# Attention with a mixture-of-experts layer on one core: softmax sums divide the pairs' outputs, their reciprocals transposed with the next pair

## The chip, the cores and the metric

The kernel runs on one core of a Trainium2 chip. Its engines run side by side, each through its own queue in program order, and wait for one another on semaphores: TensorE (PE in the profile, PEld its weight loads), VectorE (DVE), ScalarE (ACT), GpSimd (POOL) and SyncE (SP), which only issues transfers. The metric is the time of one execution on the device in microseconds, the median of three runs.

## The reference

For x of shape (8, 256, 128), all in fp32, the result is x + attention(xn) + experts(xn), with xn the layer norm of x. What matters here is the attention part:

```python
sim = einsum('bhid,bhjd->bhij', q, k) * 8 + slopes * bias   # 16 heads of 64, j over 2 null keys + 256
sim = where(causal, -neg, sim)
attn = softmax(sim, axis=-1)
out = einsum('bhij,bhjd->bhid', attn, v)
out = out.transpose(0, 2, 1, 3).reshape(b, n, h * dh) @ Wout
```

q comes from a second layer norm of xn, k and v from xn itself; q and k are scaled to unit length. The expert part is a shared expert and the two best of eight experts for each token.

## The kernel before

There are four stages. Up to about 90 us the inputs are loaded, weights are transposed and split into a high and a low part (so that three reduced-precision matmuls replace one in fp32), tokens are routed, and POOL scatters them to expert slots in HBM. Up to about 180 us the experts run over 40 tiles. Then comes the attention loop over 8 batches of 256 tokens (written out for the first and the last, a hardware loop for the six between), which takes two thirds of the span, and a drain of 9 slots.

A batch has 16 slots, one for each head h. The function entry is written once for each engine and goes through the slots s; head_at(part, s, lag) gives the head that an engine works on in slot s at a given lag. Heads come in pairs (p = h // 2). For head h:
- PE, slot h (even only): scores of both heads of the pair into banks 0 and 1 (L1095).
- DVE, slot h: adds the bias, takes the row minimum of the negated scores (L902).
- ACT, slot h+1: exponential, with the row sum into den (L658). It waits also for the null copies of the pair two before.
- DVE, slot h+2: reciprocal of the sums (L882), and two scalings of the probabilities by it (L886), for the rows of the two token tiles.
- POOL, slot h+2 (odd only): copies the probabilities of the two null keys aside for the pair (L493), after the norm work of that slot.
- PE, slot h+3: three transpositions of the scaled probabilities into bank 2 (even head) or 3 (odd) (L1086), ahead of the scores of its slot. DVE (L894) or ACT (L646) copies 384 columns to probT.
- PE, slot 2p+5: probabilities times values of the pair into bank 4 (L1076, L1077).
- ACT and DVE, slot 2p+6: split of that output into a high part (L638) and a low part (L877).
- PE, slot 2p+7: output projection by three matmuls (helper three, L953 to L955), summed over the pairs in bank 6.

Beside the heads, each slot holds up to two side jobs of the lists JOBS: "kq" (projections of keys or queries of the next batch, 128x512), "tr" (their transposition, L1041), "v" (values), "sh" (shared expert), "pn" (null probabilities transposed), "yt" (result transposed and summed with the gathered expert rows). A kq job goes from PE in slot s to ACT (L596, L597), DVE (L863, L867) and POOL in slot s+1: POOL raises to the power -0.5 (L424 for keys; L427 and L430 for queries) and scales 128x512 (L440). Such jobs stand in PE's slots 1, 4, 5, 6, 7, 11, 12 and 13, so in POOL's slots 2, 5, 6, 7, 8, 12, 13 and 14. POOL also splits inputs into two parts in slots 0, 1 and 2 (L455, L458, L475, L478) and the shared expert's product in slots 7 and 10 (L466, L468), and in slot 10 it waits for the end of the batch before (fin) and issues four gathers of expert rows (L504).

The order on POOL within a slot is: input splits, norm work, null copies, gathers. The slots' order on each engine is that of the program text; nothing reorders it.

## Time and profile before

| | |
|---|---|
| median of 3 runs | 546.41 us (544.74 to 547.65) |
| the profiled execution | 547.41 us, span 545.5 us, mean granted clock 0.951 |
| PE busy | 432.8 us (79%) |
| DVE busy | 406.6 us (75%) |
| ACT busy | 364.5 us (67%) |
| POOL busy | 327.7 us (60%) |
| attention loop | from about 182 us to the end |

Busy PE time uses modelled ends, since matmuls overlap. The granted clock of TensorE has two levels here, 1.00 (2.4 GHz) and 0.50 (1.2 GHz). In a timeline row "[1.40 <-DVE nmx L902]" says that the engine stood idle for 1.40 us before the instruction and what ended it. POOL's durations are rough.

### The profile page before, as it was taken

What the parts mean: (1) busy time and instruction counts of PE and PEld (TensorE: products, weight loads), DVE (VectorE), ACT (ScalarE), POOL (GpSimd) and SP (SyncE); (2) the same over time, 40 slices, a digit from 0 to 9 for tenths busy, and PEclk for the clock granted to TensorE, in tenths of its full rate; (3) what the DMA queues carried; (4) which work ended last, traced back from release to release, by engine and by line L of the source; (5) the groups of instructions that cost most, each with busy time, mean ns of one, the idle gap of its engine ahead of it and who ended that gap; (6) DMA issues with size and microseconds to landing.
All of it is one profiled execution on the core that took longest, in us unless ns stands there. A gap on an engine that the chain in (4) does not pass through costs nothing.

```text
span 545.5 us, 12308 instructions
## 1 busy us (share of the span) xinstructions
PE 432.8 (79%) x2867; PEld 319.2 (59%) x2868; DVE 406.6 (75%) x1469; ACT 364.5 (67%) x1096; POOL 327.7 (60%) x492
## 2 busy tenths in 40 slices
PE   0657243888888789987997998999799899889895
PEld 0656121667666557665765766666576566567663
DVE  3855532655554499989988998898898899888885
ACT  1343132566555778886895887888588688769854
POOL 2276778910000478867957867786796787677140
PEclk9999666999999999999998998999899899989989
DMA  7931112122221000001000000100000000010010
GB/s 221 351 113 40 38 48 68 40 70 63 61 59 51 18 0 22 2 2 29 11 0 19 19 0 0 38 0 0 24 15 0 19 19 0 0 37 2 3 40 10
DMA packets 28586, 21.17 MB, mean 39 GB/s; under 512 B 3560, under 2 KB 25744, under 8 KB 28432
## 3 DMA queue, kind: packets, MB, share of 16 engines
q1 hardware_dynamic: 25696, 16.65, 10.3%
q0 software_dynamic: 2048, 4.20, 2.6%
q8 instruction: 10, 0.16, 0.1%
q10 hardware_dynamic: 816, 0.03, 0.1%
q14 instruction: 16, 0.13, 0.1%
HBM read 12.48 MB, written 8.39 MB: 38 GB/s over the span
## 4 chain that ended last, share of the span: by engine, by line
POOL 27%; PE 27%; issue 21%; DVE 15%; ACT 4%; DMA 3%; POOLq 1%; SPq 1%; DVEq 1%; ACTq 0%
POOL slot_x L414 6%; POOL rnorm L424 6%; PE bank L953 4%; POOL arena_b L504 4%; POOL rpow L427 4%; DVE arena_b L902 3%; PE bank L955 3%; PE bank L954 3%; DVE arena_b L886 3%; PE bank L1171 3%; POOL pnull L493 2%; PE bank L1095 2%; DMA arena_b<-in_L_ffn_wu_dram 2%; PE bank L1142 2%; PE bank L1150 2%
## 5 line engine op out<-in xcount | busy, mean ns | idle before, releaser
L658 ACT ACTIVATE arena_b<-arena_b,nmx 128x130 f32<-128x130 f32 (+1 forms) x256 | 115.1, 458 | 27.9 <-DVE nmx L902 19.9
L886 DVE TENSOR_SCALAR arena_b<-arena_b,rden 128x130 f32<-128x130 f32 (+1 forms) x256 | 102.4, 444 | 4.6
L902 DVE CUSTOM_DVE_ANT_0 arena_b<-bank,bias 128x130 f32<-128x130 f32 (+1 forms) x256 | 81.0, 353 | 17.7 <-PE bank L1095 9.9
L1095 PE MATMUL bank<-arena_a 64*128 64x130 f32 (+1 forms) x512 | 60.6, 356 | 23.0 <-DVE nmx L902 22.0
L427 POOL TENSOR_TENSOR rpow<-ssm,mhalf 128x8 f32<-128x8 f32 x32 | 52.7, 1647 | 40.5 <-DVE ssm L867 40.5
L1086 PE MATMUL bank<-ident,arena_b 128*128 128x128 f32 x384 | 67.5, 285 | 7.0 <-DVE arena_b L886 6.9
L440 POOL TENSOR_TENSOR arena_b<-arena_b,rnorm 128x512 f32<-128x512 f32 x64 | 67.1, 1048 | 8.4 <-POOL rnorm L430 3.8
L596 ACT ACTIVATE arena_b<-bank 128x512 f32<-128x512 f32 x64 | 38.2, 597 | 32.9 <-PE bank L955 32.2
L424 POOL TENSOR_TENSOR rnorm<-ssm,mhalf 128x8 f32<-128x8 f32 x32 | 52.5, 1641 | 7.7 <-DVE ssm L867 7.6
L1095 PEld LDWEIGHTS bank<-arena_a 64*128 64x128 f32 x512 | 34.1, 189 | 35.8 <-DVE nmx L902 29.8
L863 DVE TENSOR_REDUCE ssq<-arena_b 128x8 f32<-128x512 f32 x64 | 43.4, 678 | 15.6 <-ACT arena_b L596 15.2
L1086 PEld LDWEIGHTS bank<-ident,arena_b 128*128 128x128 f32 x384 | 42.3, 141 | 20.7 <-DVE arena_b L886 12.0
L658 ACT ACTIVATION_READ_ACCUMULATOR arena_b<-arena_b,nmx 128x1 f32 x256 | 50.8, 198 | 0.0
L455 POOL CAST arena_r<-xn2T 128x256 fp32r (+1 forms) x8 | 3.1, 393 | 70.8 <-PE bank L955 70.8
L894 DVE COPY probT<-bank 128x384 f32<-128x384 f32 x64 | 35.5, 555 | 12.6 <-PE bank L1086 9.8
L1076 PE MATMUL bank<-probT,arena_a 128*64 128x256 f32 x256 | 44.0, 418 | 0.8 <-DVE arena_r L877 0.8
L1041 PE MATMUL bank<-ident,arena_b 128*128 128x128 f32 x256 | 39.8, 280 | 4.4 <-ACT arena_a L605 2.8
L414 POOL DMA_INDIRECT slot_x<-arena_a,slot x32 | 32.7, 1021 | 15.6 <-issue 9.2
L504 POOL DMA_INDIRECT arena_b<-slot_y,slot_now x32 | 31.8, 993 | 14.0 <-issue 7.3
L1041 PEld LDWEIGHTS bank<-ident,arena_b 128*128 128x128 f32 x256 | 29.6, 141 | 16.2 <-issue 9.5
L597 ACT ACTIVATE arena_b<-bank 128x512 f32<-128x512 f32 x64 | 38.1, 596 | 0.0
L925 DVE SCALAR_TENSOR_TENSOR arena_b<-arena_b,bank 128x256 f32<-128x256 f32 x40 | 16.9, 421 | 27.6 <-ACT arena_b L695 27.3
(210 smaller groups left out, 1128.9 us busy)
## 6 DMA issues: line engine op xcount, KB each, us to landing
slot_x<-probT SPq DMA_DIRECT2D x4, 640.0 KB, 7.7
arena_b<-slot_x SPq DMA_DIRECT2D x40, 64.0 KB, 1.8
slot_y<-arena_b SPq DMA_DIRECT2D x40, 64.0 KB, 1.6
arena_b<-in_L_ffn_wd_dram SPq DMA_DIRECT2D x1, 1024.0 KB, 9.9
arena_b<-in_L_attn_Wkv_dram SPq DMA_DIRECT2D x1, 1024.0 KB, 8.6
arena_b<-in_L_attn_x_dram SPq DMA_DIRECT2D x8, 128.0 KB, 2.2
out_dram<-arena_b SPq DMA_DIRECT2D x8, 128.0 KB, 1.8
arena_b<-in_L_attn_Wq_dram SPq DMA_DIRECT2D x1, 512.0 KB, 6.4
```

Of the source, the lines that this page charges most:

```text
L414: pool.indirect_dma_start(xg_dram, bass.IndirectOffsetOnAxis(ap=slot[:, n // TOPK, n % TOPK:n % TOPK + 1], axis=0), xn1[:, n // TOPK, :], ...
L424: gp.tensor_tensor(rnorm[:, j, :], ssm[:, j, :], mhalf[:, 0:HEADS // 2], ALU.pow).then_inc(g.r_ready, 1)
L427: gp.tensor_tensor(rpow[:, j, :], ssm[:, j, :], mhalf[:, 0:HEADS // 2], ALU.pow).then_inc(g.pw, 1)
L440: gp.tensor_tensor(rows, rows, bc(rnorm[:, j, :], DH), ALU.mult).then_inc(g.kqn, 1)
L504: pool.indirect_dma_start(yg[:, t, c, :], None, yg_dram, bass.IndirectOffsetOnAxis(ap=slot_now[:, t, c:c + 1], axis=0)).then_inc(g.gath, 16)
L658: sc.activation(prob[:, h % 4, c], sim[h % 2][:, c], ACT.Exp, scale=-1.0, bias=nmx[:, h % HEADS, t:t + 1], accum_out=den[:, h % HEADS, t:t ...
L886: ve.tensor_scalar(pr, pr, rden[:, h % HEADS, t:t + 1], None, ALU.mult).then_inc(g.pn, 1)
L902: ve.tensor_tensor_reduce(out=sim[h % 2][:, c], in0=bank[h % 2][:, c], in1=bias[:, c], scale=-SLOPES[h], scalar=3e38, op0=ALU.add, op1=ALU ...
L1041: ins = te.transpose(side[i][:, q * P:(q + 1) * P], src[:, p * P:(p + 1) * P], ident[:])
L1076: te.matmul(opair[r, 0:SEQ], v[:, 0, hh * DH:(hh + 1) * DH], probT[half][:, 0:SEQ], start=True, stop=False)
L1086: ins = te.transpose(bank[2 + h % 2][:, k * P:(k + 1) * P], prob[:, h % 4, c:c + P], ident[:])
L1095: ins = te.matmul(bank[half][:, c0:c1], qT[r, h // 2, q0:q0 + P], kT[r, h // 2, 0:c1 - c0], start=True, stop=True)
```

## The change

The scalings of the probabilities (L886) go. The transposed probabilities stay unscaled, and the pair's output is multiplied by the reciprocals instead. Since in that output the rows are features and the columns tokens, the reciprocals have to be spread over 64 rows and transposed: POOL widens them to 128x256 (rwide, one new copy for each pair), and PE transposes these with the next pair's probabilities, into the fourth 128 columns of banks 2 and 3 (function turned). The copies of these banks grow from 384 to 512 columns, and probT has two buffers of both halves. The multiplication by DVE takes the place of its subtraction; ACT's evacuation (L638) goes, and the output projection becomes one fp32 matmul with unsplit weights (wo), so that the split of these weights before the loop goes too.

In order: the transpositions come one slot earlier (lag 2) and behind the scores of their slot; the DVE copy of bank 2 comes last in its slot; one reciprocal of 128x4 serves a pair; POOL's widening and null work stand ahead of the norm work of their slot, and the null copies become multiplications by the reciprocals. New waits: PE's transpositions for the widening of the pair before (rw), DVE's multiplication for the copies of the next pair.

```diff
@@ -60,7 +60,7 @@
-        wo = [sb("wo_hi", [P, PAIRS, DIM], F32R), sb("wo_lo", [P, PAIRS, DIM], F32R)]
+        wo = sb("wo", [P, PAIRS, DIM])
...
@@ -118,7 +117,7 @@
-        probT = [sb(f"probT{i}", [P, 3 * P]) for i in range(2)]
+        probT = sb("probT", [P, 2, 2, 4 * P])
...
@@ -132,7 +131,8 @@
         rt[0] = 4 * SEQ
-        oT = [[carve_r(SEQ), carve_r(SEQ)] for _ in range(2)]
+        oT = [sb(f"oT{i}", [P, SEQ]) for i in range(2)]
+        rwide = [sb(f"rwide{i}", [P, SEQ]) for i in range(2)]
         hss = [carve_r(2 * I), carve_r(2 * I)]
...
@@ -294,6 +294,15 @@
+        def turned(part, s):
+
+            h = head_at(part, s, 2)
+            if part == "first" and h in (0, 1):
+                return h, slice(0, 3 * P)
+            if part == "drain" and s in (2, 3):
+                return s - 2, slice(3 * P, 4 * P)
+            return h, slice(0, 4 * P)
+
         groups = [([raw_gu[:, w, 2 * e + c, :] for w in range(2) for c in range(2)],
...
@@ -478,20 +487,27 @@
                     h = head_at(part, s, 2)
-                    for _, job_b, job in (behind(part, b, s, 1) if part != "ahead" else []):
-                        norms(job_b, job)
-                        scale_by_norm(job_b, job)
                     if h is not None and h % 2:
                         p = h // 2
-                        pool.wait_ge(g.pn, TB * (HEADS * b + h + 1))
+                        pool.wait_ge(g.rd, PAIRS * b + p + 1)
+                        if part != "first" or p >= 2:
+                            pool.wait_ge(g.ptps, HEADS * b + 2 * p)
+                        settled(pool)
+                        gp.tensor_copy(rwide[p % 2][:].rearrange("p (t h d) -> p t h d", t=TB, d=DH),
+                                       rden[:, 2 * (p % PAIRS):2 * (p % PAIRS) + 2, :].rearrange("p h t -> p t h").unsqueeze(3)
+                                       .to_broadcast([P, TB, 2, DH])).then_inc(g.rw, 1)
                         if p == 0 and part != "first":
                             pool.wait_ge(g.pn_hi, 2 * b)
                         settled(pool)
                         q = p % PAIRS
                         two = prob[:, h % 4 - 1:h % 4 + 1, :]
                         for t, c0 in ((0, 0), (1, K0)):
-                            gp.tensor_copy(pnull[:, t, 4 * q:4 * q + 4].rearrange("p (h n) -> p h n", n=2),
-                                           two[:, :, c0:c0 + NNULL]).then_inc(g.pnc, 1)
+                            gp.tensor_tensor(pnull[:, t, 4 * q:4 * q + 4].rearrange("p (h n) -> p h n", n=2),
+                                             two[:, :, c0:c0 + NNULL], bc(rden[:, 2 * q:2 * q + 2, t], NNULL),
+                                             ALU.mult).then_inc(g.pnc, 1)
+                    for _, job_b, job in (behind(part, b, s, 1) if part != "ahead" else []):
+                        norms(job_b, job)
+                        scale_by_norm(job_b, job)
                     if s == 10 and "own" in whose:
...
@@ -556,9 +572,7 @@
             sc.activation(lth, lg, ACT.Tanh, scale=0.5).then_inc(g.lth_ready, 1)
-            act.wait_ge(g.o_in, 16)
             sc.activation(wkv[0][:], raw_w[:, INNER:3 * INNER], ACT.Copy).then_inc(g.wraw_hi, 1)
-            sc.activation(wo[0][:], raw_o, ACT.Copy).then_inc(g.wraw_hi, 1)
             act.wait_ge(g.small_in, 16 * 9)
...
@@ -629,21 +643,15 @@
                 for s in steps:
-                    h = head_at(part, s, 5)
-                    if h is not None and h % 2:
-                        p = h // 2
-                        act.wait_ge(g.pvd, PAIRS * b + p + 1)
-                        if part != "first" or p >= 2:
-                            act.wait_ge(g.oread, PAIRS * b + p - 1)
-                        sc.activation(oT[p % 2][0], opair, ACT.Copy).then_inc(g.ohi, 1)
                     for job in behind(part, b, s, 1):
                         side_out(*job)
-                    h = head_at(part, s, 3)
+                    h, cols = turned(part, s)
                     if h is not None and h % 2 == 1:
+                        p = h // 2
                         act.wait_ge(g.ptps, HEADS * b + h + 1)
-                        if part != "first" or h >= 2:
-                            act.wait_ge(g.pvd, PAIRS * b + h // 2)
-                        sc.activation(probT[1][:], bank[3][:, 0:3 * P], ACT.Copy).then_inc(g.ptev_a, 1)
+                        if part != "first" or p >= 2:
+                            act.wait_ge(g.pvd, PAIRS * b + p - 1)
+                        sc.activation(probT[:, p % 2, 1, cols], bank[3][:, cols], ACT.Copy).then_inc(g.ptev_a, 1)
                     if s == 6 and "prev" in whose:
...
@@ -814,11 +822,9 @@
                 split_group(n)
-            dve.wait_ge(g.wraw_hi, 3)
+            dve.wait_ge(g.wraw_hi, 2)
             ve.tensor_tensor(wq[1][:], raw_w[:, 0:INNER], wq[0][:].bitcast(F32), ALU.subtract).then_inc(g.wraw_lo, 1)
             ve.tensor_tensor(wkv[1][:], raw_w[:, INNER:3 * INNER], wkv[0][:].bitcast(F32), ALU.subtract).then_inc(g.wraw_lo, 1)
-            ve.tensor_tensor(wo[1][:], raw_o, wo[0][:].bitcast(F32), ALU.subtract).then_inc(g.wraw_lo, 1)
-
...
@@ -873,25 +879,20 @@
                         p = h // 2
-                        dve.wait_ge(g.ohi, PAIRS * b + p + 1)
-                        ve.tensor_tensor(oT[p % 2][1], opair, oT[p % 2][0].bitcast(F32),
-                                         ALU.subtract).then_inc(g.olo, 1)
+                        dve.wait_ge(g.pvd, PAIRS * b + p + 1)
+                        dve.wait_ge(g.ptev_a, PAIRS * b + p + 2)
+                        dve.wait_ge(g.ptev_d, PAIRS * b + p + 2)
+                        if part != "first" or p >= 2:
+                            dve.wait_ge(g.oread, PAIRS * b + p - 1)
+                        ve.tensor_tensor(oT[p % 2][:].rearrange("p (t q) -> p t q", q=P), opair.rearrange("p (t q) -> p t q", q=P),
+                                         probT[:, (p + 1) % 2, :, 3 * P:4 * P], ALU.mult).then_inc(g.odone, 1)
                     h = head_at(part, s, 2)
-                    if h is not None:
+                    if h is not None and h % 2:
                         dve.wait_ge(g.exp, TB * (HEADS * b + h + 1))
-                        ve.reciprocal(rden[:, h % HEADS, :], den[:, h % HEADS, :]).then_inc(g.rd, 1)
-                        dve.wait_ge(g.rd, HEADS * b + h + 1)
-                        for t, c in ((0, slice(0, K0)), (1, slice(K0, KS))):
-                            pr = prob[:, h % 4, c]
-                            ve.tensor_scalar(pr, pr, rden[:, h % HEADS, t:t + 1], None, ALU.mult).then_inc(g.pn, 1)
-                    h = head_at(part, s, 3)
+                        hh = slice((h - 1) % HEADS, (h - 1) % HEADS + 2)
+                        ve.reciprocal(rden[:, hh, :], den[:, hh, :]).then_inc(g.rd, 1)
                     for job in behind(part, b, s, 1):
                         side_out(*job)
-                    if h is not None and h % 2 == 0:
-                        dve.wait_ge(g.ptps, HEADS * b + h + 1)
-                        if part != "first" or h >= 2:
-                            dve.wait_ge(g.pvd, PAIRS * b + h // 2)
-                        ve.tensor_copy(probT[0][:], bank[2][:, 0:3 * P]).then_inc(g.ptev_d, 1)
                     h = head_at(part, s, 0)
...
@@ -902,6 +903,13 @@
                                                     accum_out=nmx[:, h, t:t + 1]).then_inc(g.ttr, 1)
+                    h, cols = turned(part, s)
+                    if h is not None and h % 2 == 0:
+                        p = h // 2
+                        dve.wait_ge(g.ptps, HEADS * b + h + 1)
+                        if part != "first" or p >= 2:
+                            dve.wait_ge(g.pvd, PAIRS * b + p - 1)
+                        ve.tensor_copy(probT[:, p % 2, 0, cols], bank[2][:, cols]).then_inc(g.ptev_d, 1)
...
@@ -1069,22 +1077,14 @@
                         if part != "first" or p >= 1:
-                            pe.wait_ge(g.olo, PAIRS * b + p)
+                            pe.wait_ge(g.odone, PAIRS * b + p)
                         for half, evacuated in ((0, g.ptev_d), (1, g.ptev_a)):
                             pe.wait_ge(evacuated, PAIRS * b + p + 1)
                             r, hh = slice(half * DH, (half + 1) * DH), 2 * (p % PAIRS) + half
-                            te.matmul(opair[r, 0:SEQ], v[:, 0, hh * DH:(hh + 1) * DH], probT[half][:, 0:SEQ], start=True, stop=False)
-                            ins = te.matmul(opair[r, P:SEQ], v[:, 1, hh * DH:(hh + 1) * DH], probT[half][:, SEQ:3 * P],
+                            te.matmul(opair[r, 0:SEQ], v[:, 0, hh * DH:(hh + 1) * DH], probT[:, p % 2, half, 0:SEQ], start=True, stop=False)
+                            ins = te.matmul(opair[r, P:SEQ], v[:, 1, hh * DH:(hh + 1) * DH], probT[:, p % 2, half, SEQ:3 * P],
                                             start=False, stop=True)
                         ins.then_inc(g.pvd, 1)
-                    h = head_at(part, s, 3)
-                    if h is not None:
-                        pe.wait_ge(g.pn, TB * (HEADS * b + h + 1))
-                        if part != "first" or h >= 2:
-                            pe.wait_ge(g.ptev_a if h % 2 else g.ptev_d, PAIRS * b + h // 2)
-                        for k, c in enumerate((NNULL, K0 + NNULL, K0 + NNULL + P)):
-                            ins = te.transpose(bank[2 + h % 2][:, k * P:(k + 1) * P], prob[:, h % 4, c:c + P], ident[:])
-                        ins.then_inc(g.ptps, 1)
                     h = head_at(part, s, 0)
...
@@ -1095,6 +1095,20 @@
                         ins.then_inc(g.sps, 2)
+                    h, cols = turned(part, s)
+                    if h is not None:
+                        if part != "first" or h >= 2:
+                            pe.wait_ge(g.ptev_a if h % 2 else g.ptev_d, PAIRS * b + h // 2)
+                        if cols.start == 0:
+                            pe.wait_ge(g.exp, TB * (HEADS * b + h + 1))
+                            for k, c in enumerate((NNULL, K0 + NNULL, K0 + NNULL + P)):
+                                ins = te.transpose(bank[2 + h % 2][:, k * P:(k + 1) * P], prob[:, h % 4, c:c + P], ident[:])
+                        if cols.stop == 4 * P:
+                            p = h // 2 - 1
+                            pe.wait_ge(g.rw, PAIRS * b + p + 1)
+                            ins = te.transpose(bank[2 + h % 2][:, 3 * P:4 * P],
+                                               rwide[p % 2][:, h % 2 * P:(h % 2 + 1) * P], ident[:])
+                        ins.then_inc(g.ptps, 1)
                     for job in todo:
...
@@ -1105,9 +1119,9 @@
                             pe.wait_ge(g.yev, b)
-                        pe.wait_ge(g.olo, PAIRS * b + p + 1)
-                        three(bank[6][:, 0:SEQ], [x[:, p % PAIRS, :] for x in wo], oT[p % 2], p == 0,
-                              p == -1).then_inc(g.oread, 1)
+                        pe.wait_ge(g.odone, PAIRS * b + p + 1)
+                        te.matmul(bank[6][:, 0:SEQ], wo[:, p % PAIRS, :], oT[p % 2][:], start=p == 0,
+                                  stop=p == -1).then_inc(g.oread, 1)
                     if s == 13 and "own" in whose:
```

## Rows read from the trace of the kernel before

The slots of the rows: the marker at 295.98 is POOL's slot 8 of a middle batch; on PE, 304.94 is the kq job of slot 12, 325.71 to 326.51 that of slot 4 of the next batch, 337.99 the scores of slot 8 and 345.40 those of slot 10.

**Rows 1.** Windows: busy us of PE, PEld, DVE, ACT, POOL; clock, DMA share, GB/s.

```profile
300.00:350.00 50.00, 45.38 (x327) 32.82 (x323) 45.01 (x171) 39.95 (x124) 37.67 (x57) 0.97 0.04 12
```

**Rows 2.** Timeline of POOL: start us, us, line, operation, tiles, count, idle before.

```profile
204.49 1.64 POOL L427 TENSOR_TENSOR rpow<-ssm,mhalf 128x8 f32<-128x8 f32 x1
...
295.98 1.64 POOL L427 TENSOR_TENSOR rpow<-ssm,mhalf 128x8 f32<-128x8 f32 x1 [1.58 <-DVE ssm L867]
...
305.69 0.94 POOL L504 DMA_INDIRECT arena_b<-slot_y,slot_now  x1 [0.31 <-issue]
...
328.40 1.64 POOL L427 TENSOR_TENSOR rpow<-ssm,mhalf 128x8 f32<-128x8 f32 x1 [3.35 <-DVE ssm L867]
...
332.65 1.64 POOL L424 TENSOR_TENSOR rnorm<-ssm,mhalf 128x8 f32<-128x8 f32 x1 [0.80 <-DVE ssm L867]
...
335.44 0.40 POOL L466 CAST arena_r<-arena_b 128x256 fp32r<-128x256 f32 x1
...
336.95 1.64 POOL L424 TENSOR_TENSOR rnorm<-ssm,mhalf 128x8 f32<-128x8 f32 x1 [0.31 <-DVE ssm L867]
...
341.86 1.64 POOL L427 TENSOR_TENSOR rpow<-ssm,mhalf 128x8 f32<-128x8 f32 x1 [1.58 <-DVE ssm L867]
...
479.53 1.64 POOL L427 TENSOR_TENSOR rpow<-ssm,mhalf 128x8 f32<-128x8 f32 x1 [1.58 <-DVE ssm L867]
```

**Rows 3.** Timeline of PE, the same columns, two batches.  

```profile
304.94 0.50 PE L953 MATMUL bank<-wkv_hi,arena_r 128*128 128x512 f32 x1
...
317.77 0.50 PE L953 MATMUL bank<-wq_hi,arena_r 128*128 128x512 f32 x1 [0.49 <-POOL arena_r L458]
...
323.16 0.65 PE L1041 MATMUL bank<-ident,arena_b 128*128 128x128 f32 x4 [0.39 <-ACT arena_a L605]
...
324.85 0.93 PE L1095 MATMUL bank<-arena_a 64*128 64x130 f32 x8 [0.36 <-DVE nmx L902]
...
326.51 0.40 PE L953 MATMUL bank<-wkv_hi,xs_late 128*128 128x512 f32 x1
...
336.04 0.55 PE L1086 MATMUL bank<-ident,arena_b 128*128 128x128 f32 x3 [0.63 <-DVE arena_b L886]
337.99 1.66 PE L1095 MATMUL bank<-arena_a 64*128 64x130 f32 x8 [1.40 <-DVE nmx L902]
...
345.40 0.93 PE L1095 MATMUL bank<-arena_a 64*128 64x130 f32 x8 [1.34 <-DVE nmx L902]
```

**Rows 4.** Groups by line and shape: busy us, mean ns of one, idle before.

```profile
L1086 PE MATMUL bank<-ident,arena_b 128*128 128x128 f32 x384 | 67.5, 285 | 7.0 <-DVE arena_b L886 6.9
L440 POOL TENSOR_TENSOR arena_b<-arena_b,rnorm 128x512 f32<-128x512 f32 x64 | 67.1, 1048 | 8.4 <-POOL rnorm L430 3.8 <-POOL rnorm L424 2.8
...
L886 DVE TENSOR_SCALAR arena_b<-arena_b,rden 128x130 f32<-128x130 f32 x128 | 58.4, 456 | 4.6
...
L1076 PE MATMUL bank<-probT,arena_a 128*64 128x256 f32 x256 | 44.0, 418 | 0.8 <-DVE arena_r L877 0.8
...
L894 DVE COPY probT<-bank 128x384 f32<-128x384 f32 x64 | 35.5, 555 | 12.6 <-PE bank L1086 9.8 <-DVE pnT L839 1.3 <-DVE arena_b L833 1.2
...
L877 DVE TENSOR_TENSOR arena_r<-bank,arena_r 128x256 fp32r<-128x256 f32 x64 | 26.9, 420 | 2.4 <-ACT arena_r L638 2.4
...
L954 PE MATMUL bank<-arena_r,wo_lo 128*128 128x256 f32 x64 | 18.0, 281 | 0.0
...
L468 POOL TENSOR_TENSOR arena_r<-arena_b,arena_r 128x256 fp32r<-128x256 f32 x16 | 11.7, 731 | 1.3
...
L475 POOL CAST xs_late<-xn1T 128x256 fp32r x6 | 2.4, 395 | 0.0
```

**Rows 5.** PE busy time, then granted clock, in short stretches.

```profile
86.00:91.00 5.00, 0.00 (x0) 0.50 0.17 54
335.00:338.00 3.00, 0.96 (x9) 1.00 0.00 0
338.00:341.00 3.00, 3.00 (x11) 0.50 0.00 0
```

15 lines of the change are left out of this document (7 added, 8 removed).

## The prediction

> **What bounds the kernel now.** Read the windows first. In the attention loop VectorE (DVE) is busy for 45.0 of 50 us, TensorE (PE) for 45.4 by modelled ends, ScalarE for 40.0 and POOL for 37.7 [rows 1]: no engine is full, and three are close. So the bound is a chain that changes engines, and it has to be found in the timelines. The marker I use is POOL's inverse-norm operation of slot 8 (L427). It comes at 204.49 us in the first batch, at 295.98 and 341.86 in two middle ones and at 479.53 in the seventh [rows 2]: six periods in 275.04 us, 45.84 us each. One period is 16 slots, so 2.87 us per slot.
>
> Next, who stops PE in a period [rows 3]. Small stops come at 317.77 (POOL), 323.16 (ScalarE) and 324.85 (DVE); the large ones are 0.63 us before 336.04, 1.40 before 337.99 and 1.34 before 345.40, all three put down to DVE, in slots 7 to 10, where DVE also adds the gathered expert rows. In the middle of them the granted clock falls to 0.50 for 3 us of full work [rows 5]: the scores at 337.99 take 1.66 us instead of 0.93 at 345.40 [rows 3], and of 3 us at half speed up to 1.5 are lost. DVE is thus what ends last in slots 5 to 10. POOL is what ends last nowhere yet, but it runs from slot 8 to slot 2 nearly without idling: four gathers start after the marker and the last ends at 305.69 + 0.94 = 306.63, which is 10.65 us after it [rows 2].
>
> **DVE and ScalarE.** DVE loses four scalings and one of two reciprocals a pair. The short half of the scalings takes 0.456 us [rows 4], the long one about the same, so 4 x 0.45 = 1.8 us; with the reciprocal 1.95. The subtraction (0.420) becomes a multiplication of the same shape, and the copy of 384 columns (0.555) one of 512: a third more at most, 0.19 [rows 4]. Net -1.75 us a pair, 14 us a batch out of 41. ScalarE loses one evacuation of 256 columns a pair and widens another by a third. Neither addition lies on a path; both engines now have slack, and DVE's three stops of PE in slots 7 to 10 should go, but for about a microsecond around the gathered rows, which stay. The splitting of the output weights before the loop (L561, L820) is 1 us on each engine while POOL is still scattering tokens: nothing.
>
> **PE.** Added are 16 transpositions a batch. Four in a row take 0.65 us [rows 3], one alone 0.285 [rows 4], so one more costs (0.65 - 0.285) / 3 = 0.12 at most; I take 0.11. Three reduced-precision matmuls of 256 columns, 0.12 apart, 0.35 in all, become one in full precision, which the trace records as two passes. A pass of 256 columns there takes 0.418 against 0.281 for a reduced one of the same width [rows 4], 0.14 more: 0.52 to 0.56 by that, 0.43 if the columns simply take twice as long. I take +0.1 a pair (bounds 0.05 and 0.2). Sum: 16 x 0.11 + 8 x 0.1 = 2.6 us a batch. PE's own work was 45.84 less its stops; the six of [rows 3] sum to 4.6, about 0.2 more each start to start (a stop is counted from the modelled end of the last matmul) makes 5.8, and 1.4 of clock 7.2, so 38.7. It becomes 41.3. PE alone would allow a period of 41.3.
>
> **POOL.** Each pair gets a widening copy of 128x256, and its two null copies become multiplications of the same four columns (0.02 more each). The trace has no such copy with a broadcast source. Nearest: the cast of 128x256 at 0.395 and, with two inputs, the subtraction at 0.731; a multiplication with a broadcast operand, 128x512, takes 1.048, no more per column than one without [rows 4]. A broadcast is thus free and I take 0.38 beside its neighbours, bounds 0.38 and 0.73. Eight of them: 3 us a batch. Its idle time in the period is at least 6.0 us (the four places of [rows 2]), so its own load is at most 39.8, and at least 37.7 x 45.84 / 50 = 34.6 [rows 1]; short gaps between dependent operations belong to it, so I take 39, and it becomes 42.
>
> The Trainium skill (GPSIMD Engine Reference, section Performance versus the Vector engine) speaks against moving work there: elementwise work belongs on VectorE, and POOL needs about 2.6 cycles per element for two inputs. By that figure a widening would be an estimated 0.55 us, between my bounds; rows of one-input operations here lie below it.
>
> **The new wait, and what is queued behind it.** The transposition of head h (even or odd) now also turns the widened reciprocals of the pair before, so PE in slot 12 waits for POOL's widening of pair 4, which stands in POOL's slot 11, behind the four gathers of slot 10. Before, nothing of slot 12 on PE waited for POOL; the null copies were needed only two slots later. All of PE's later work queues behind that wait, and DVE's copy of the bank with it. This closes a ring through POOL and PE. Its legs, from marker to marker:
> - POOL, marker to widening of pair 4: 10.65 + two widenings (pairs 3 and 4) 0.76 + 0.1 = 11.5 us. PE used to be through the scores of slot 12 at 304.94, 8.96 after the marker: it now starts this point 2.55 later.
> - PE from there to the end of the key/query job of slot 4 (next start 326.51): 326.51 - 304.94 = 21.57, less the three stops, 1.24 as shown and 1.7 start to start: 19.85. One more turning in this stretch than before 0.4, nine transpositions 1.0, four output matmuls 0.4: 21.6.
> - squaring, reduction, until POOL's L427 at 328.40: 1.9 [rows 2, 3].
> - POOL from 328.40 to 341.86: 13.46, less its idle of 0.80, 0.31 and 1.58 [rows 2] = 10.8. Pair 1's null copies move ahead of this stretch and pair 2's widening comes in, even. The stretch starts with work whose inputs are there earlier than now, since DVE no longer delays them.
>
> Sum: 11.5 + 21.6 + 1.9 + 10.8 = 45.8 us, against 45.84. The change thus trades the 2.7 us of POOL's waits for DVE against 2.55 us of a wait for the gathers, and PE's gain against PE's added work.
>
> **The clock.** In this ring PE has nothing to do for about 45.8 - 41.3 = 4.5 us in a batch, some 1.2 of it in slot 10 (end of the gathered-row work, widening of pair 3) and some 3 in one piece before the wait in slot 12. Where PE stood with nothing, the granted clock was 0.50 (from 86 to 91 us, busy 0), and in slots 7 to 8 it fell to 0.50 after 3 us with 0.96 busy [rows 5]. I expect the same at the new stop, and now at the head of the leg where PE sets the pace. Its price lies between 0 and 1.5 us; part of the slow stretch may be spent standing, so I take 1.2. Period 47.0, +1.2.
>
> **The ends.** Before the first marker the last leg shrinks a little: -0.6. After the seventh: late by 2.55 + 0.6, clock 1.2; then 16 slots and the drain without POOL's load, added PE work 2.6, stops gone 3.4 less 1, clock 1.4 back, shorter chain at the end about 1 (no scaling before the last transposition): 6.95 - 4.8 = +2.1, without the clock +0.9; some smaller stops go too, so I take +1 and -0.4.
>
> **How the numbers follow.** The profiled execution takes 547.4 us (span 545.5), 1.0 above the median of the three runs, 546.4; I apply differences to the median. About 0.5% (2.7 us) is what a measurement of this kernel can tell from no change.
> - Forecast, ring with lowered clock: -0.6 + 6 x 1.15 + 1 = +7.3, so 553.7; I give 553.5 us, own range 549 to 558. Chance 0.43.
> - Rival 1, the clock holds (the stop is shorter than 3 us, or split): -0.6 + 6 x -0.1 - 0.4 = -1.6, with a spread of 3: 545, range 541 to 548. For it: the stop is a difference of large numbers, and the stop of 1.34 us before 345.40 was at full clock. Chance 0.29.
> - Rival 2, faster: the gathers aren't what ends last in slot 12. This decides if POOL reaches its slot 11 before PE its slot 12, so if the marker comes 3 us earlier against PE than I count, for DVE feeds it sooner. Then POOL's load bounds, 42 to 43.5 us: 6 x -3 - 1.5 = about -20, 527. Against it: POOL's slots 5 to 8 are themselves dense, 10.8 us of work for four slots. Chance 0.17.
> - Rival 3: the widening costs two-input price, 0.35 more, three in the ring: 1.05 a period, 6.3 more: 560. Chance 0.11.
>
> Range 537 to 560: it leaves out rival 2 and the top of rival 3. Faster by over 0.5% (under 543.7): rival 2 and half of rival 1, 0.32; within: the rest of rival 1 and the low edge of the forecast, 0.21; slower 0.47.
>
> **What would show it.** Right: PE's first matmul after the scores of slot 12 waits 2 to 4 us for POOL's widening, followed by a stretch at clock 0.5; markers 46.5 to 47.5 apart; no idle on POOL from slot 5 to the gathers; DVE near 30 of 50 us; no large stop of PE for DVE in slots 7 and 8. Wrong: markers 42 to 44 apart with only short waits for POOL (rival 2), the clock at 1.00 in slots 12 and 13 (rival 1), a widening above 0.6 us (rival 3). A matmul of the output weights above 0.6 us, or ScalarE as the engine that PE waits for, would overturn the PE leg.

## The result, and the profile after

The changed kernel takes 556.58 us, median of 4 runs (555.09 to 558.56), beside 546.32 us for the kernel before in the same comparison: ratio 1.019, 95% interval 1.014 to 1.024. It is slower; whether by more than 2% the interval leaves open. The predicted 553.5 us was 3 us short of it.

The page of the changed kernel, its first part (busy us, share of the span, instructions) and the clock row of its second:

```profile
span 556.8 us, 12270 instructions
...
PE 448.2 (81%) x2931; PEld 326.0 (59%) x2932; DVE 318.1 (57%) x1149; ACT 351.5 (63%) x1032; POOL 348.3 (63%) x556
...
PEclk9857566999999999998999899899999989989989
```

DVE has lost 88 us of work and the kernel takes 10 us more. So DVE's load was not what the time hung on. POOL gained 21 us.

The markers (POOL's rpow of slot 8, now L436; columns as in [rows 2]), in two neighbouring middle batches and the seventh:

```profile
344.37 1.64 POOL L436 TENSOR_TENSOR rpow<-ssm,mhalf 128x8 f32<-128x8 f32 x1
...
391.76 1.64 POOL L436 TENSOR_TENSOR rpow<-ssm,mhalf 128x8 f32<-128x8 f32 x1
...
484.95 1.64 POOL L436 TENSOR_TENSOR rpow<-ssm,mhalf 128x8 f32<-128x8 f32 x1
```

The first marker stands at 203.79, so the six periods take 281.16 us, 46.86 each on average, and what follows the last takes 71.85. Against [rows 2] the 11.3 us of span divide into three terms: up to the first marker -0.70, six periods +6.12, behind the seventh marker +5.88. A second pair of traces (e5 and e6 below, the same two kernels again) gives 0.0, +7.4 and +5.6, so the first term is not to be told from nothing, and the second is known to little better than a microsecond.

Inside a batch, POOL from its marker on (timeline; the first number is the start, the second the duration):

```profile
347.44 0.40 POOL L496 COPY rwide<-rden 128x256 f32<-128x256 f32 x1
...
349.37 0.19 POOL L515 COPY w_now<-wts 128x4 f32 x1
350.38 1.08 POOL L520 DMA_INDIRECT arena_b<-slot_y,slot_now  x1 [0.83 <-POOL w_now L515]
351.77 0.95 POOL L520 DMA_INDIRECT arena_b<-slot_y,slot_now  x1 [0.30 <-issue]
353.03 0.95 POOL L520 DMA_INDIRECT arena_b<-slot_y,slot_now  x1 [0.30 <-issue]
354.28 0.95 POOL L520 DMA_INDIRECT arena_b<-slot_y,slot_now  x1 [0.30 <-issue]
355.23 0.40 POOL L496 COPY rwide<-rden 128x256 f32<-128x256 f32 x1
```

and PE in the same stretch:

```profile
341.32 0.93 PE L1095 MATMUL bank<-arena_a 64*128 64x130 f32 x8 [0.78 <-DVE nmx L903]
...
347.63 0.93 PE L1095 MATMUL bank<-arena_a 64*128 64x130 f32 x8 [1.53 <-DVE nmx L903]
...
352.47 0.93 PE L1095 MATMUL bank<-arena_a 64*128 64x130 f32 x8
...
355.69 0.33 PE L1109 MATMUL bank<-ident,rwide 128*128 128x128 f32 x1 [1.82 <-POOL rwide L496]
```

The scores of slot 12 (352.47) and three transpositions behind them are done, and PE stands for 1.82 us until the widening that starts at 355.23, right behind the fourth gather. This is the wait of the forecast, in its place. Over the whole loop (two rows of the list of waits, from 200 to 560 us: us in total, times, longest us):

```profile
PE bank L1095 <- DVE nmx L903: 16.0, 16, 1.6
PE bank L1109 <- POOL rwide L496: 15.4, 8, 2.8
```

Behind the stop the clock falls (windows: from:to, us, busy us of PE, PEld, DVE, ACT, POOL, granted clock, DMA share, GB/s):

```profile
355.00:358.00 3.00, 2.31 (x14) 1.63 (x16) 1.31 (x3) 1.16 (x3) 2.78 (x6) 0.86 0.08 22
358.00:360.00 2.00, 2.00 (x12) 1.57 (x9) 1.52 (x6) 0.81 (x2) 1.98 (x5) 0.50 0.00 0
360.00:361.00 1.00, 1.00 (x7) 0.76 (x6) 0.42 (x1) 1.00 (x5) 1.00 (x1) 0.71 0.00 0
...
404.00:409.00 5.00, 5.00 (x40) 3.85 (x38) 3.48 (x11) 4.67 (x12) 4.68 (x8) 1.00 0.00 0
```

The fall is in four of the six periods, which are 47.34 to 47.39 us long; the other two are 45.82 and 45.85, though their stops are no shorter (2.81 and 1.82 us). The last window is one of these two: behind the stop that ends at 403.09 the clock stays at 1.00.

### The profile page after: what moved, and what is told of

Read it like the earlier page. It is cut to its first block, busy times and chain, and to the rows that moved or that the text cites. A ratio compares the mean times of both kernels' runs of the same rounds, so it can differ in the third digit from the quotient of the medians.

```text
span 556.8 us, 12270 instructions
## 1 busy us (share of the span) xinstructions
PE 448.2 (81%) x2931; PEld 326.0 (59%) x2932; DVE 318.1 (57%) x1149; ACT 351.5 (63%) x1032; POOL 348.3 (63%) x556
## 4 chain that ended last, share of the span: by engine, by line
PE 40%; POOL 26%; issue 16%; ACT 7%; DVE 5%; DMA 4%; POOLq 1%; SPq 1%; ACTq 0%; DVEq 0%
POOL slot_x L423 6%; POOL arena_b L520 5%; POOL rnorm L433 5%; PE bank L961 4%; PE bank L1105 4%; PE bank L1095 4%; PE bank L963 4%; PE bank L962 4%; PE bank L1084 3%; PE bank L1185 3%; PE bank L1049 3%; POOL rpow L436 3%; ACT arena_b L666 3%; POOL arena_b L449 2%; DMA arena_b<-in_L_ffn_wu_dram 2%
## 5 line engine op out<-in xcount | busy, mean ns | idle before, releaser
L666 ACT ACTIVATE arena_b<-arena_b,nmx 128x130 f32<-128x130 f32 (+1 forms) x256 | 113.9, 452 | 2.7 <-DVE nmx L903 2.7
L1105 PE MATMUL bank<-ident,arena_b 128*128 128x128 f32 x384 | 71.6, 296 | 1.8 <-ACT arena_b L666 1.8
L654 ACT ACTIVATE probT<-bank 128x512 f32<-128x512 f32 (+2 forms) x65 | 38.5, 592 | 49.1 <-PE bank L1109 49.0
L610 ACT ACTIVATE arena_b<-bank 128x512 f32<-128x512 f32 x64 | 37.7, 588 | 40.4 <-PE bank L963 40.3
L436 POOL TENSOR_TENSOR rpow<-ssm,mhalf 128x8 f32<-128x8 f32 x32 | 52.8, 1649 | 14.9 <-DVE ssm L873 14.3
L1105 PEld LDWEIGHTS bank<-ident,arena_b 128*128 128x128 f32 x384 | 40.7, 143 | 35.2 <-issue 30.4
L912 DVE COPY probT<-bank 128x512 f32<-128x512 f32 (+2 forms) x65 | 44.0, 677 | 12.8 <-PE bank L1109 12.7
L496 POOL COPY rwide<-rden 128x256 f32<-128x256 f32 x64 | 25.6, 399 | 39.7 <-DVE rden L893 39.6
L1109 PE MATMUL bank<-ident,rwide 128*128 128x128 f32 x128 | 36.1, 282 | 15.5 <-POOL rwide L496 15.4
L887 DVE TENSOR_TENSOR oT<-bank,probT 128x256 f32<-128x256 f32 x64 | 27.0, 422 | 36.5 <-ACT probT L654 22.3
L1049 PE MATMUL bank<-ident,arena_b 128*128 128x128 f32 x256 | 40.7, 285 | 2.2 <-ACT arena_a L619 1.1
```

Of the source, the lines that this page charges most:

```text
L436: gp.tensor_tensor(rpow[:, j, :], ssm[:, j, :], mhalf[:, 0:HEADS // 2], ALU.pow).then_inc(g.pw, 1)
L666: sc.activation(prob[:, h % 4, c], sim[h % 2][:, c], ACT.Exp, scale=-1.0, bias=nmx[:, h % HEADS, t:t + 1], accum_out=den[:, h % HEADS, t:t ...
L912: ve.tensor_copy(probT[:, p % 2, 0, cols], bank[2][:, cols]).then_inc(g.ptev_d, 1)
L1049: ins = te.transpose(side[i][:, q * P:(q + 1) * P], src[:, p * P:(p + 1) * P], ident[:])
L1105: ins = te.transpose(bank[2 + h % 2][:, k * P:(k + 1) * P], prob[:, h % 4, c:c + P], ident[:])
```

## Experiments

Each kernel ran beside the kernel before on the same chip, on three chips in all. On the first chip (e1 to e4) the kernel before took 553.63 us; on the others 546.04 (e5 to e8) and 546.45 (e9 to e11). The kernel of e1 does not show this difference (it took 531.84 there and 532.58 on the third chip), so for e1 to e4 I read the absolute times and the markers first. There is no trace of the kernel before from that chip, and what slowed it stays open.

### Are the gathers what PE waits for?

**e1.** The changed kernel, with the gathers apart:

```diff
+GATHERS = [('own', 10, 0), ('own', 15, 1), ('prev', 3, 2), ('prev', 4, 3)]
...
-                        for t in range(TB):
-                            for c in range(TOPK):
-                                pool.indirect_dma_start(yg[:, t, c, :], ...
+                    for whose_k, s_k, k in GATHERS:
+                        if s == s_k and whose_k in whose:
+                            t, c = k // TOPK, k % TOPK
+                            pool.indirect_dma_start(yg[:, t, c, :], ...
```

> The changed kernel, with POOL's four gathers of slot 10 spread: one stays in slot 10, one goes to slot 15, two to slots 3 and 4 of the next batch. Nothing else moves. Theory R (a ring: PE's transpositions of slot 12 wait for POOL's widening of pair 4, which stands behind the gathers): the widening comes 3.8 us earlier after the marker, PE no longer stops 1.8 us in slot 12, the clock stays at 1.00 there, periods fall from 46.9 to 43.5 to 44.5 us, where PE's own 41.3 plus its stops for the gathered-row work bound; 538 to 543 us in all. Theory W (the added work on PE, 16 transpositions and full-precision projections, sets the time, and PE would stop elsewhere): periods stay above 46, 553 us or more.

Measured: 531.84 us, some 25 less than the changed kernel and 14 less than the kernel before elsewhere, and 6 us under the expected range. Five of the six periods are 43.8 us, as expected, and the first 42.8; what follows the seventh marker fell as well, from 71.85 to 64.8 us, and that had not been counted. The clock row of the page is full through the loop. PE's only two stops of a period (timeline of PE, 334.3 to 378.2) are:

```profile
337.58 0.93 PE L1097 MATMUL bank<-arena_a 64*128 64x130 f32 x8 [1.55 <-DVE nmx L905]
...
375.04 0.93 PE L1097 MATMUL bank<-arena_a 64*128 64x130 f32 x8 [0.78 <-DVE nmx L905]
```

The stop for POOL in slot 12 is gone, and POOL's widening comes 7.1 us after its marker instead of 10.9:

```profile
334.33 1.64 POOL L437 TENSOR_TENSOR rpow<-ssm,mhalf 128x8 f32<-128x8 f32 x1
...
340.33 1.07 POOL L522 DMA_INDIRECT arena_b<-slot_y,slot_now  x1 [0.82 <-DVE rden L895]
341.42 0.41 POOL L497 COPY rwide<-rden 128x256 f32<-128x256 f32 x1
```

What stays doubtful is the ratio (0.961, interval 0.958 to 0.964), since its kernel before was slow. **e10** is the same kernel again:

> The changed kernel with all gathers apart in every batch, a second time, on another chip (the first time it took 531.8 us beside a kernel before of 553.6, while the kernel before took 546 elsewhere). If the kernel's time is a property of the kernel and the first chip's time for the kernel before was the odd one: 530-533 us, ratio 0.970-0.977. If the first chip made every kernel slower by as much: 524-527 us, ratio 0.961.

Measured: 532.58 us, ratio 0.975, interval 0.972 to 0.977, periods as in e1. The first reading holds: the kernel's time is its own. This version is faster than the kernel before by 2.5%, and than the changed one by some 24 us.

**e4.** The same edit in the kernel before:

> The kernel before with the same spreading of the gathers. Theory R: there only the null copies stand behind the gathers and they are needed two slots later, so little changes, 541 to 547 us. If the gathers' place were worth as much without the change, it would gain as much as the changed kernel does from it, 15 us.

Measured: 543.01 us, markers 45.45 apart on average. Against 546.4 elsewhere that is 3.4 less; against its neighbour 10.6 less (0.982, interval 0.977 to 0.986). The markers speak for the small value: 0.4 us a period. (That the kernel before has its usual markers on this chip is not shown.) Taking the gathers apart is worth 3 us in the kernel before and 25 in the changed one, so what the change added is the dependence on them.

**e2.** The other way round, the dependence alone, in the kernel before:

```diff
                     h = head_at(part, s, 0)
...
                         ins.then_inc(g.sps, 2)
+                    if s == 12 and "own" in whose:
+                        pe.wait_ge(g.pnc, 2 * (PAIRS * b + 5))
```

> The kernel before with one added wait alone: PE in slot 12, after the scores, waits for POOL's null copies of pair 4, which stand behind the gathers in slot 11. No work is added. Theory R: PE resumes 11.1 us after the marker instead of passing at 9.0, and the rest of the period does not shrink, so periods rise from 45.8 to 47 to 48 and the time to 553 to 560 us. Theory W: PE has slack, at most 549 us.

Measured: 562.06 us, ratio 1.016, interval 1.011 to 1.020; against 546.4 elsewhere 15.7 more. Markers 47.8 apart on average: 46.8 in the two periods without a fall of the clock behind the wait, 48.3 in the four with one. So the wait costs 0.9 us by itself, against the 45.9 of the kernel before, and a fall behind it 1.5 more. Waits of PE:

```profile
PE bank L1095 <- DVE nmx L902: 18.7, 17, 1.4
PE bank L953 <- issue: 14.2, 7, 2.2
```

The second row is the added wait, 2.0 us in each of seven batches. One wait, with no other part of the change, makes the kernel before as slow as the changed one and slower: the ring is enough as a cause. (The 562 lie 2 above the expected range; this kernel also keeps DVE's stops, and its clock falls to a mean of 0.93 over 300 to 350 us.)

### Is the clock a cost of its own?

**e3.** Work without use keeps PE busy through the stop:

```diff
                             p = h // 2 - 1
+                            if s == 12 and "own" in whose:
+                                for _ in range(14):
+                                    te.transpose(bank[2][:, 3 * P:4 * P], ident[:], ident[:])
                             pe.wait_ge(g.rw, PAIRS * b + p + 1)
```

> The changed kernel with 14 transpositions of the identity in slot 12, between PE's own transpositions and its wait for the widening, into the block that is overwritten afterwards: 1.5 us of filling where PE stands for 1.8 to 2.0. Theory R with the clock in the ring: the clock stays at 1.00 in slots 12 and 13, periods of 47.4 become 45.9 as the one of 45.85 that the trace shows without a fall, 547 to 550 us. If the lowered clock costs nothing because others are late anyway: 556 us or a little above.

Measured: 548.82 us (5 runs), 8 to 10 below the changed kernel. All six periods are 45.8 us. The clock row of its page, over the same 40 slices as before:

```profile
PEclk9999666999999999999999999999999999999999
```

The ring still closes in the same way: PE's turning of the widened reciprocals starts 11.31 us after the marker, as in the changed kernel (11.32), right behind the widening, though the profile puts the 0.28 us that PE still stands there down to "issue". Only the clock changed. So of the ring's 46.9 to 47.1 us a period, 1.0 to 1.3 on average are the clock. And the ring without the clock is as long as the period before, as the sum of the legs had it.

### Does DVE's late work still matter?

**e8.** e1's kernel, with DVE's sums over the gathered rows moved from the head of slot 8 behind the scores' minima and the copy of that slot:

```diff
-                    for k, (src, dst) in enumerate(((z0, z1), (z1, z2))):
+                if kind == "yrest":
+                    for k, (src, dst) in enumerate(((z0, z1), (z1, z2))):
...
+                    for job_part, job_b, job in behind(part, b, s, 1):
+                        if job[0] == "yt":
+                            side_out(job_part, job_b, ("yrest", *job[1:]))
```

> The kernel of e1 (gathers spread), and DVE adds the gathered rows (two pairs of 128x128 operations, L862) at the end of its slot 8 instead of ahead of slot 8's scores; only the first addition, which frees the bank, stays ahead. In e1 PE's last stops are 0.78 and 1.54 us in slots 8 and 10, for DVE. Theory R (what is left is PE's work and these stops): both shrink, periods fall from 43.8 to 42.2 to 43.2, where POOL's load of 42 binds next, 4 to 10 us less than e1's 0.961 of the kernel before, so 0.943 to 0.953 of it. If PE is held by its own work alone: no change against e1.

Measured: 533.45 us, ratio 0.977, interval 0.975 to 0.979: no gain over e1 or e10. The reason is in DVE's timeline (e8):

```profile
335.21 1.25 DVE L865 SCALAR_TENSOR_TENSOR arena_b<-arena_b,w_now 128x128 f32<-128x128 f32 x4
336.38 0.17 DVE L896 RECIPROCAL rden<-den 128x4 f32<-128x4 f32 x1
336.47 0.39 DVE L838 SCALAR_TENSOR_TENSOR arena_b<-arena_b,bank 128x256 f32<-128x256 f32 x1
336.90 0.42 DVE L841 SCALAR_TENSOR_TENSOR arena_b<-arena_b,bank 128x256 f32<-128x256 f32 x1
337.71 0.29 DVE L906 CUSTOM_DVE_ANT_0 arena_b<-bank,bias 128x130 f32<-128x130 f32 x1 [0.40 <-ACT arena_b L668]
```

In e1 the same stretch reads:

```profile
330.59 0.28 DVE L905 CUSTOM_DVE_ANT_0 arena_b<-bank,bias 128x130 f32<-128x130 f32 x1
332.06 1.26 DVE L864 SCALAR_TENSOR_TENSOR arena_b<-arena_b,w_now 128x128 f32<-128x128 f32 x4 [0.17 <-DVE arena_b L857]
336.88 0.29 DVE L905 CUSTOM_DVE_ANT_0 arena_b<-bank,bias 128x130 f32<-128x130 f32 x1 [0.40 <-ACT arena_b L668]
```

PE's scores of slot 8 (331.28 in e1) wait for the minimum of slot 7 (330.59), and those of slot 10 for the minimum of slot 9 (336.88 in e1, 337.71 in e8). The sums (332.06, 335.21) stand between the two in both kernels, so the edit moved them past neither. Nor do they set the stop of slot 10: with the sums early or late, DVE stands idle for 0.40 us ahead of the minimum of slot 9, for ScalarE's exponential, and PE's stops are 0.76 and 1.59 us, as in e1. ScalarE in turn had waited for PE (timeline of e8; L656 is its copy of bank 3):

```profile
336.43 0.60 ACT L656 ACTIVATE probT<-bank 128x512 f32<-128x512 f32 x1 [0.93 <-PE bank L1115]
336.93 0.39 ACT L668 ACTIVATE arena_b<-arena_b,nmx 128x130 f32<-128x130 f32 x1
```

The stop of slot 10 is thus the end of a round trip from PE's turning over ScalarE's copy and exponential and DVE's minimum back to PE. No run changed that chain.

### How much of the period is PE's output projection?

**e7.** The changed kernel with the projection as one reduced-precision matmul per pair (mean duration 0.339 us, one record instead of two). It leaves out the precision of the output projection.

```diff
-        oT = [sb(f"oT{i}", [P, SEQ]) for i in range(2)]
+        oT = [sb(f"oT{i}", [P, SEQ], F32R) for i in range(2)]
...
-                        te.matmul(bank[6][:, 0:SEQ], wo[:, p % PAIRS, :], oT[p % 2][:], start=p == 0,
+                        te.matmul(bank[6][:, 0:SEQ], wor[:, p % PAIRS, :], oT[p % 2][:], start=p == 0,
```

> The changed kernel with the output projection in reduced precision, one pass of 256 columns instead of two longer ones: it leaves out the precision of that product. About 0.4 us less PE work a pair. Theory R (only the projections between slot 12 and slot 4 count, four of eight a batch; the others end in PE's stop in slot 12): periods 1.6 us shorter, 9 to 12 us less than the changed kernel. Theory W (all of PE's work counts): 3.2 us a period, 20 us less or more.

Beside it on the same chip **e6**, the changed kernel again, and **e5**, the kernel before again:

> The changed kernel, unchanged, as the base of the runs beside it. 1.014 to 1.024 of the kernel before, periods near 47.4 where the clock falls in slot 12 and 45.9 where it does not.

> The kernel before, unchanged, for its trace on the chip of these runs. It took 553.6 us beside the runs e1 to e4 and 546.3 elsewhere. If the clock is the cause: periods of 45.8 us as before with more time at 0.50 outside the attention loop. If the loop is: longer periods.

Measured: e5 546.4 us (ratio 1.001, interval 0.999 to 1.003; its periods are 45.9 us, so this chip is not slow for the kernel before, and e5 can't tell what the first chip did to it), e6 559.17 (1.023, 1.019 to 1.027), e7 548.54 (1.004, 1.002 to 1.006). That is 10.6 us less than e6 and 8.0 less than the first measurement of the changed kernel. Not all of it is the projection's second pass: e6 has the fall of the clock behind the stop in five of its six periods (47.1 us on average), e7 in three, and a fall is worth 1.5. Like with like, a period with the fall is 46.4 us instead of 47.38, one without it 44.9 instead of 45.8: 0.9 us. All of it lies in PE's leg. From PE's start behind the stop of slot 12 to POOL's rpow of slot 5 it takes 375.40 - 352.88 = 22.52 us in e7 and 426.47 - 403.09 = 23.38 in the changed kernel, both without the fall; POOL's leg to that start is 11.3 in both, and its slots 5 to 8 are 11.13 and 11.14. Outside PE's leg the gain only lengthens stops: 1.40, 1.87 and 2.12 us in slots 8, 10 and 12 instead of 0.78, 1.53 and 1.82. So Theory R has the pairs right, those in PE's leg, and their price too high: 0.9 over four pairs is 0.23 each, since what follows a reduced pass starts 0.2 to 0.37 us after it and not 0.12.

The same trace shows when a fall costs something. In two of its periods the clock falls ahead of slot 12 (windows, then PE's timeline):

```profile
300.00:303.00 3.00, 3.00 (x16) 2.10 (x16) 1.46 (x7) 0.84 (x4) 2.08 (x8) 0.53 0.00 0
```

```profile
307.94 0.33 PE L1112 MATMUL bank<-ident,rwide 128*128 128x128 f32 x1 [0.57 <-POOL rwide L497]
```

The stop is then 0.57 us instead of 2.12 and the period 44.95, as long as the one with no fall at all (44.97): there PE would have waited for POOL anyway. The kernel before shows no cost either for its falls in slots 7 and 8: its periods are 45.9 us with such a fall and without (45.87 in e5). What the change did was to bring the fall behind the stop, onto the leg where PE sets the pace.

### Where does the growth behind the last marker come from?

**e9.** The changed kernel, gathers apart in the last batch only:

```diff
+                        for k in (range(1) if part == "last" else range(TB * TOPK)):
+                            gather(k)
+                    if s == 15 and part == "last":
+                        gather(1)
+                    if s in (3, 4) and part == "drain":
+                        gather(s - 1)
```

> The changed kernel with one edit: only in the last batch the four gathers are issued apart (the first in slot 10, one in slot 15, two in the steps 3 and 4 after the loop); the loop over the batches is left as it is. What lies behind the seventh marker was 71.9 us in the changed kernel and 66.0 in the kernel before. Theory T: this growth is the last batch's own gathers, which hold POOL and so PE in slot 12 once more and let the clock fall. Then the periods stay at 46.9 on average, what lies behind the last marker falls from 71.9 to 65-67 us, and the time is 5-6 us below that of the changed kernel: 550-553 us, ratio to before 1.007-1.013. Theory U: the growth is the extra work of the pairs at the end, not the gathers. Then the part behind the last marker stays at 70-72 and the time at 555-559.

Measured: 555.32 us, ratio 1.016, interval 1.012 to 1.020. Markers 47.11 apart, and 68.4 us behind the seventh, 3.45 less than in the changed kernel. The stop for POOL that the changed kernel has in its last batch (timeline of PE of the changed kernel) is not there, and the other stops behind it are the same (1.22, 0.36, 0.33 and 0.56 us):

```profile
536.83 0.33 PE L1109 MATMUL bank<-ident,rwide 128*128 128x128 f32 x1 [1.66 <-POOL rwide L496]
```

In e10, where the batch before the last is free of the stop too, 64.84 us follow the marker (530.7 - 465.86). The growth of 5.88 us is then: gathers of the last batch 3.45, gathers of the batch before it (its slot 12 lies behind the seventh marker) 68.4 - 64.8 = 3.6, everything else 64.84 - 65.97 = -1.1. Theory T named the cause and over-sized it: it wanted all of the growth from the last batch. The total is 1.3 us below the changed kernel's instead of 5 to 6; of the 3.45 us, the profiled execution lost 1.5 to one more period with the fall. The -1.1 is no more than two executions of the kernel before differ by behind this marker (65.97 and 64.82 us in e5), so whether everything else costs or gains there stays open.

### How steep is the ring?

**e11.** Each widening done twice, the first into a tile that nobody reads:

```diff
+                        gp.tensor_copy(rspare[p % 2][:].rearrange("p (t h d) -> p t h d", t=TB, d=DH), ...
                         gp.tensor_copy(rwide[p % 2][:].rearrange("p (t h d) -> p t h d", t=TB, d=DH),
```

> The changed kernel with one edit: POOL makes each widening copy twice, the first time into a tile that nobody reads, so each pair costs POOL 0.40 us more and nothing else changes. Ring theory: between two markers three of these copies stand on the path (pair 3 and pair 4 ahead of PE's wait in slot 12, pair 2 ahead of the next marker), so a period grows by 0.8-1.2 us, the six and the end by 6-9 us: 562-566 us, ratio to before 1.029-1.037. Load theory (POOL is what bounds everywhere): eight copies a batch, 3.2 us a period, some 22 us: 577-580. Cover theory (POOL's waits of 5 us for the reciprocals take it in): 0-2 us more, 556-559.

Measured: 570.25 us, ratio 1.045, interval 1.042 to 1.049. The stop in slot 12 is longer,

```profile
360.40 0.47 PE L1114 MATMUL bank<-ident,rwide 128*128 128x128 f32 x1 [2.68 <-POOL rwide L501]
```

and an ordinary period is 48.25 us where the changed kernel has 47.38: +0.87, in the ring's 0.8 to 1.2 and far from the load theory's 3.2. The total is over the ring's range all the same, and the clock is why: here all six periods have the fall, and one of them, 49.48 us long, a deeper one (windows):

```profile
361.00:366.00 5.00, 5.00 (x21) 3.48 (x21) 2.20 (x8) 2.09 (x4) 4.76 (x8) 0.50 0.00 0
366.00:367.00 1.00, 1.00 (x6) 0.71 (x6) 0.43 (x1) 1.00 (x6) 0.92 (x2) 0.70 0.00 0
```

Over the changed kernel's span this one has 10.5 us more: some 5.2 (six times 0.87) and 1.1 behind the last marker from the work itself, the other 4.2 from falls in the two periods that had none (3.0) and the deeper one (1.2).

## Why the prediction was right

**The bound.** Right. No engine was full; a chain through several was the bound. That DVE lost 88 us of busy time and the kernel takes 10 us more says it most plainly.

**The ring and its legs.** Right, leg by leg. Marker to the end of pair 4's widening: predicted 11.5, measured 355.63 - 344.37 = 11.26. PE from there to POOL's rpow of slot 5, squaring and clock included: predicted 21.6 + 1.9 + 1.2 = 24.7, measured 380.63 - 355.69 = 24.94. POOL's slots 5 to 8: predicted 10.8, measured 391.76 - 380.63 = 11.13. The last one begins and ends so:

```profile
380.63 1.64 POOL L436 TENSOR_TENSOR rpow<-ssm,mhalf 128x8 f32<-128x8 f32 x1 [0.42 <-DVE ssm L873]
...
388.02 0.40 POOL L496 COPY rwide<-rden 128x256 f32<-128x256 f32 x1
...
390.49 1.17 POOL L449 TENSOR_TENSOR arena_b<-arena_b,rnorm 128x512 f32<-128x512 f32 x1 [0.16 <-POOL rnorm L433]
```

Period with the clock 47.0 predicted, 47.38 measured where the clock falls and 46.86 on average; without it 45.8 and 45.8 (e3). e1, e2, e7 and e11 vary the ring from four sides and agree. "No idle on POOL from slot 5 to the gathers" held, beside gaps of 0.16 us between dependent operations, but for 0.33 us in slot 6 and the 0.83 us ahead of the first gather; the latter was in the 10.65 us of [rows 2] already.

**The clock.** Right in size, with some luck and for a reason that was partly wrong. I took 1.2 us in each period; a fall costs 1.5 and comes in four of six periods (five in e6), 1.0 on average (1.25): a price too low and a count too high offset each other. And I tied it to a stop of some 3 us (2 to 4 among the signs), and let rival 1 hold if the stop were shorter. The stop was 1.82 us, shorter, and the clock fell all the same; a stop of 2.81 us in the first batch passed without a fall. The length of the stop does not decide here. The Trainium skill (TensorE: Matmul & The Clock Gate, Part 1: The HAM clock gate) puts the full clock down to recent activity and has the point of change vary from run to run; the runs agree, with falls in five of six periods in e6 and in four of six in the profiled execution of the same kernel.

**PE's added work.** Right. The projection's two passes take 0.53 us start to start (estimated 0.43 to 0.56, taken +0.1 over 0.35: 0.45, so 0.08 a pair too little). PE's own work, predicted 41.3, is by an estimate from e10 the period of 43.79 less the two stops of 2.3 and about 0.2 more each start to start, 41.1. (The projection's cost was taken low, the rest a little high.)

**POOL.** Right. The widening takes 0.399 us, 64 times (predicted 0.38, bounds 0.38 and 0.73), so rival 3 fell. The group in the page:

```profile
L496 POOL COPY rwide<-rden 128x256 f32<-128x256 f32 x64 | 25.6, 399 | 39.7 <-DVE rden L893 39.6
```

By the rate for two inputs in the Trainium skill (GPSIMD Engine Reference, section Performance versus the Vector engine) it would have been an estimated 0.55 us; for this copy with one input the row decides. POOL's load was predicted at 42 us a batch; in e1 POOL waits 1.88 and 0.27 us for DVE in a period of 43.79, so 41.6. Spread out, POOL and PE (41.1) are equally near to setting the pace: of rival 2's 42 to 43.5 us e1 reached 43.8, and 532 us where 527 was the estimate, though by another way than rival 2's: the gathers had to be moved.

**DVE's stops of PE.** DVE is busy for 31.6 of 50 us, near the 30 expected, but its stops were wrong in size, without effect. I let the 3.4 us of stops in slots 7 to 10 shrink to about 1.2; the changed kernel has 0.78 and 1.53, 2.3 in all. I put what would be left down to the gathered rows; that was wrong. The stop in slot 10 stands behind ScalarE's exponential (e8), which the relief of DVE did not reach, and ahead of the stop in slot 8 DVE has a sum of squares and its scaling to do for the kq job before the minimum (339.29 to 340.6 in the changed kernel; no run varied this one). In the ring a stop ahead of slot 12 only shortens the stop in slot 12 (e7 shows the exchange), so they cost nothing: stops were 4.5 us a period in the prediction, and 0.78 + 1.53 + 1.82 = 4.1 in the trace. Without the ring (e1) they are what is left to gain.

**The ends.** This is the term that was mis-sized. Up to the first marker -0.70 (predicted -0.6), a match by luck: traces of one kernel differ there by 0.6. Behind the seventh I took +1, with the words "without POOL's load": but the last batch is freed of the next batch's norm work only, not of its own gathers. POOL issues them at 531.53 to 536.4, PE stands 1.66 us, and the clock falls again:

```profile
535.00:540.00 5.00, 3.34 (x20) 2.57 (x19) 2.13 (x9) 1.46 (x6) 2.49 (x8) 0.81 0.11 29
540.00:545.00 5.00, 4.55 (x31) 3.12 (x30) 2.06 (x12) 2.12 (x9) 0.71 (x3) 0.85 0.00 0
```

That is 3.45 us by e9. The rest of the term was nearly as counted: 3.6 for the batch before it where I had 2.55 + 0.6 + 1.2, and -1.1 (or 0.0 against e5) where I had -2.2. With the sum of its own items (+2.1) and 3.45 more it would have been 5.6, against 5.88 measured. The forecast had 7.3 of the 11.3 us of span; this term was 4.9 short, and the periods came out 0.8 shorter in sum than forecast.

## What to carry to other kernels

When a change gives an engine that leads (here TensorE) a new wait on an engine that runs behind, cost what stands in front of the awaited instruction in that queue, not the instruction: here a copy of 0.4 us stood behind four gather issues of 1.25 us each, and that made some 25 us of difference. The same rows tell the remedy, which is worth more than the change itself: put the issues apart so that no row of them stands before a short operation on which another engine waits (532 us against 546 and 557). And count a wait once for each time its pattern occurs, in the batches written out at the ends too.

## What the runs showed of the hardware

- An indirect gather of 128 rows occupies POOL for 0.95 us, with 0.30 us more before the next one, and there is 0.83 us between the copies ahead of it and the first: 5.7 us for the four, in which nothing else on POOL runs. The Trainium skill (GPSIMD Engine Reference, section Key points) sends indirect gathers to this engine, and the traces agree as to where they run; the issue time is what the traces add.
- TensorE's granted clock fell to 0.50 while PE was fully busy, 0.4 to 1.5 us after it had resumed (0.86 as the mean of 355 to 358; 0.67 in the microsecond from 449, where PE had resumed at 448.93), in batches whose rows up to there equal those of batches in which it held 1.00 (stops of 1.82 us at 355.69 and at 403.09). Behind the stop a fall cost 1.5 us (47.38 against 45.85 us), ahead of it nothing (44.95 against 44.97 in e7); in e11, where the stop is 2.68 us, one lasted some 6 us, and that period was 1.2 us longer than its neighbours.
- Fp32 transpositions of the identity, with no other use, kept the clock at 1.00 through the stop and paid for themselves (e3, 8 to 10 us).
- Freeing DVE hardly shortened what waits for it: DVE went from 45 to 31.6 of 50 us busy, and PE's stops for it from 3.4 to 2.3 us a batch.
- A copy with a broadcast source on POOL, 128x256 in fp32, takes 0.399 us, as long as the plain cast of that shape (0.395, [rows 4]).
